# One PSUM bank of the attention stage handed from the score ring to the transposed-score ring

## The chip, the cores and the metric

The kernel runs on one core of one Trainium2 chip. The metric is the device time of one execution in microseconds (us); lower is better. The engines are TensorE (PE; PEld is its weight load), VectorE (DVE), ScalarE (ACT), GpSimd (POOL) and SyncE (SP), which issues the DMAs.

## What is computed

One pre-norm transformer block on x of shape (2, 1024, 512), fp32: attention with 16 heads of 32, rotary embedding and a causal mask, then a gated feed-forward with an inner width of 1408.

```python
def _L0_attn_ref(x, Wq, bq, Wk, bk, Wv, bv, Wo, bo):
    Q = proj(Wq, bq); K = proj(Wk, bk); V = proj(Wv, bv)
    Q = Q * cos + _rotate_half(Q) * sin
    K = K * cos + _rotate_half(K) * sin
    scores = jnp.einsum('bhqd,bhkd->bhqk', Q, K) / scale
    scores = jnp.where(causal, scores, jnp.float32(-jnp.inf))
    attn = jax.nn.softmax(scores, axis=-1)
    out = jnp.einsum('bhqk,bhkd->bhqd', attn, V)
    return out.transpose(0, 2, 1, 3).reshape(B, S, H) @ Wo.T + bo
...
x = x + _L0_attn_ref(_layernorm(x, axis=-1), ...)
x = x + _L0_ffn_ref(_layernorm(x, axis=-1), ...)
```

## The kernel before, in words

The program has three stages. Stage A (chunks of 512 tokens, four of them) normalises, transposes and projects to Q, K and V, rotates Q and K, and writes them to DRAM split into high and low parts. The attention stage goes over 32 heads (2 batches of 16). Stage C makes the output projection and the feed-forward.

In attention each head's scores are computed twice. First the plain scores, queries on partitions: `score_bank(u, i)` (L1034, matmul L1050) makes bank entry i of head u, and VectorE takes the row maximum out of it in `max_piece` (L769; L783 where the causal mask cuts it, L785 where not). A head has 12 entries: 0 to 4 are 512 columns wide, entry 5 (`M_ENTRY`) is no scores but the place of the transpose of the negated maxima (`transpose_max`, L1055), 6 to 8 are 384 wide, 9 and 10 are 256 wide and 11 holds two pieces of 256. `negate_max` (L789) turns the maxima of a head into 16 columns of `neg_max` in three small steps, placed behind entries 0, 1 and 2 of the next head; ScalarE copies the transposed maxima out (L663) and two DMAs put them beside the head's Q as extra contraction rows.

Second the transposed scores, keys on partitions, with the maximum already subtracted by those extra rows: `shifted_piece(t, i)` (L1116, matmul L1124) makes piece i of head t (12 pieces, 256 to 512 wide), and ScalarE takes the exponential out of it into `p32` (`exp_piece`, L645, activation L649). GpSimd clears the diagonal blocks (L529). `output_products` (L1127, matmul L1143) then multiplies p by V for a pair of heads; a pair's 24 matmuls stand in four groups of 8, 4, 6 and 6, called G0 to G3 here. In the profile each of them shows as two records, so G0 is "x16", G1 "x8", G2 and G3 "x12". ScalarE copies the accumulated outputs out of bank 7 (L656).

The order on TensorE is written out by hand in `b_step(t)` (L1148): for i from 0 to 11 it issues the score entry i of head t+2 (or the transpose of the maxima at i = 5), then the transposed piece i of head t, and after i = 3 and i = 9 a group of output products of the pair before. G0 and G1 stand in an even step t, G2 and G3 in an odd one. So between two groups TensorE issues either the entries 4 to 9 ("the middle stretch") or the entries 10 and 11 of one step and 0 to 3 of the next ("the long stretch"). In the first chunk of work, `early` (L1063, L804) puts the scores of heads 0 and 1 between the last products of stage A.

PSUM has eight banks of 512 fp32 columns. In attention the score entries go round `S_RING` banks from `S_BANK`, the transposed pieces round `ST_RING` banks from `ST_BANK`, and bank 7 holds the outputs. Each ring is guarded by a wait on TensorE ahead of the matmul, and whatever stands behind the waiting instruction waits too: entry i of the scores waits until VectorE is done with entry i - S_RING, piece i of the transposed scores until ScalarE is done with piece i - ST_RING:

```python
                elif i >= S_RING:
                    pe.wait_ge(s_max, NS * u + s_before(i - S_RING) + 1)
...
                if t > 0 or i >= ST_RING:
                    pe.wait_ge(exp_done, NPC * t + i - ST_RING + 1)
```

The transposed maxima lie in the score ring too (`M_BANK`); the entry that comes into that bank next, number 5 + S_RING, waits for ScalarE's copy of them (`max_T`, L1040). `transpose_max` waits for the entry that was in the bank ahead of it (L1058).

Of the kernel before, what the change touches and what calls it, by code (L numbers as in the profile page):

```python
# [109 lines left out]
def transformer_block(nc, x, wq, wk, wv, wo, bqk, bv, bo, ffn, gs, us, ds, cos, sin, shift_rows, out):  # L110
    ctx = ExitStack()
    with ctx:
# [99 lines left out]

        ps = ctx.enter_context(nc.psum_tensor("ps", [P, 8, 512], F32))
        T_BANK, MM_BANK, FLAG_BANK = 0, 4, 5
        S_BANK, ST_BANK, O_BANK = 0, 4, 7
        S_RING, ST_RING = 4, 3
        M_BANK = S_BANK + M_ENTRY % S_RING


# [1076 lines left out]
```

## Time and profile before

| what | value |
|---|---|
| median of 3 runs | 792.36 us (786.74 to 794.88) |
| the profiled execution, its own time | 785.66 us |
| its span, first to last instruction | 784.0 us |
| granted TensorE clock, mean over the span | 0.991 of full speed |
| PE busy | 740.0 us (94%) |
| PEld busy | 538.9 us (69%) |
| DVE busy | 436.1 us (56%) |
| ACT busy | 301.5 us (38%) |
| POOL busy | 243.2 us (31%) |

The span and the views of the trace belong to the profiled execution; 1.7 us of its time lie outside the span. Matmul records of the trace overlap, since each has a start, a streaming time and a drain; how fast TensorE goes is read from the distance between starts, not from the durations.

### The profile page before, as it was taken

How to read it: one execution, taken by the hardware profiler on the slowest of the kernel's cores; microseconds unless marked ns; L12 is line 12 of the kernel's file. 1: busy time of each engine (PE TensorE's matmuls, PEld its weight loads, DVE VectorE, ACT ScalarE, POOL GpSimd, SP SyncE). 2: the span in 40 equal slices, each digit the busy share in tenths (PEclk: the TensorE clock that was granted, in tenths of full speed). 3: DMA queues.
4: the chain of work that ended last, by engine and by line, in shares of the span. 5: the costliest groups of instructions: out<-in, count | busy, mean ns of one | idle time of the engine just before them, and what ended most of it. 6: DMA issues, size and time to landing. Idle time of an engine off the chain costs nothing.

```text
span 784.0 us, 10619 instructions
## 1 busy us (share of the span) xinstructions
PE 740.0 (94%) x3521; PEld 538.9 (69%) x3521; DVE 436.1 (56%) x1103; ACT 301.5 (38%) x637; POOL 243.2 (31%) x222
## 2 busy tenths in 40 slices
PE   3989899998999999999999998998999999999996
PEld 3768687876555555555555545887888888888885
DVE  6846575678777777777777733794114214214112
ACT  3231313137555555555555564222222223223221
POOL 0333333431113241414141415851123223123223
PEclk9999999999999999999999999999999999999998
DMA  8275479454557665757565545680001001001001
GB/s 275 85 265 215 162 246 309 187 196 138 153 161 185 160 179 154 188 157 190 154 186 152 139 124 165 228 348 2 0 1 54 1 0 54 0 0 54 1 0 56
DMA packets 52013, 104.37 MB, mean 133 GB/s; under 512 B 14821, under 2 KB 15333, under 8 KB 51445
## 3 DMA queue, kind: packets, MB, share of 16 engines
q1 hardware_dynamic: 51960, 103.72, 43.2%
q8 instruction: 27, 0.44, 0.2%
q14 instruction: 26, 0.20, 0.1%
HBM read 69.62 MB, written 38.21 MB: 138 GB/s over the span
## 4 chain that ended last, share of the span: by engine, by line
PE 79%; DVE 6%; issue 5%; ACT 4%; DMA 3%; SPq 1%; POOL 1%; ACTq 0%; DVEq 0%; POOLq 0%
PE ps L1026 32%; PE ps L1143 17%; PE ps L1219 10%; PE ps L1050 9%; PE ps L1124 9%; ACT p L649 1%; PE ps L1018 1%; DMA x_st<-in_x 1%; ACT o_raw L656 1%; DMA us_sb<-in_us 1%; DVE x L960 1%; ACT xT_hi L575 1%; DVE stats L969 1%; DVE oT_lo L933 1%; DVE xn L745 0%
## 5 line engine op out<-in xcount | busy, mean ns | idle before, releaser
L649 ACT ACTIVATE p<-ps 128x384 f32<-128x384 f32 (+3 forms) x384 | 162.2, 489 | 124.5 <-PE ps L1124 124.1
L783 DVE CUSTOM_DVE_ANT_0 masked<-ps,mask_qk 128x512 bf16<-128x512 f32 (+1 forms) x240 | 115.4, 503 | 74.8 <-PE ps L1050 72.2
L1124 PE MATMUL ps<-q_st,k_st 99*128 99x384 f32 (+2 forms) x384 | 135.6, 371 | 6.7 <-ACT p L649 6.6
L1143 PE MATMUL ps<-p,v_slot 128*64 128x512 f32 (+3 forms) x768 | 137.5, 493 | 2.2 <-ACT o_raw L656 2.1
L1050 PE MATMUL ps<-k_st,q_st 96*128 96x512 f32 (+2 forms) x384 | 131.3, 363 | 1.1 <-DVE row_max L783 0.9
L985 DVE SCALAR_TENSOR_TENSOR hid<-ps,us_sb,silu 128x512 f32<-128x512 f32 x44 | 33.0, 750 | 169.0 <-PE ps L1026 166.5
L560 POOL TENSOR_TENSOR hid_lo<-hid,hid_hi 128x512 fp32r<-128x512 f32 x44 | 56.8, 1290 | 175.2 <-ACT hid_hi L720 175.2
L529 POOL TENSOR_SCALAR_AFFINE_SELECT p<-p 128x512 f32<-128x512 f32 x64 | 40.5, 635 | 208.7 <-ACT p L649 208.5
L1143 PEld LDWEIGHTS ps<-p,v_slot 128*64 128x64 f32 x768 | 52.6, 136 | 74.6 <-issue 61.8
L1050 PEld LDWEIGHTS ps<-k_st,q_st 96*128 96x128 f32 x384 | 72.9, 191 | 30.3 <-issue 21.6
L1124 PEld LDWEIGHTS ps<-q_st,k_st 99*128 99x128 f32 x384 | 72.9, 191 | 26.3 <-ACT p L649 15.9
L785 DVE TENSOR_REDUCE row_max<-ps 128x1 f32<-128x512 f32 (+1 forms) x128 | 83.1, 651 | 0.1
L1026 PE MATMUL ps<-xT_hi,wg_sb 128*128 128x512 f32 x176 | 68.6, 390 | 2.9 <-DVE x L960 2.9
L1219 PE MATMUL ps<-wd_sb,hid_hi 128*128 128x512 f32 x176 | 69.1, 393 | 0.0
L1219 PE MATMUL ps<-wd_sb,hid_lo 128*128 128x512 f32 x176 | 68.5, 389 | 0.0
L1026 PE MATMUL ps<-xT_lo,wg_sb 128*128 128x512 f32 x176 | 68.5, 389 | 0.0
L1026 PE MATMUL ps<-xT_lo,wu_sb 128*128 128x512 f32 x176 | 68.5, 389 | 0.0
L1026 PE MATMUL ps<-xT_hi,wu_sb 128*128 128x512 f32 x176 | 68.5, 389 | 0.0
L717 ACT ACTIVATE silu<-ps,gs_sb 128x512 f32<-128x512 f32 x44 | 30.4, 690 | 88.6 <-PE ps L1026 88.6
L499 POOL TENSOR_TENSOR rot<-ecos,osin 128x512 f32<-128x512 f32 x16 | 28.0, 1747 | 109.4 <-DVE ocos L840 109.4
L720 ACT CAST hid_hi<-hid 128x512 fp32r<-128x512 f32 x44 | 27.4, 623 | 83.1 <-DVE hid L985 83.1
L606 ACT CAST st_hi<-rot 128x1024 fp32r<-128x1024 f32 x16 | 17.0, 1060 | 88.8 <-POOL rot L500 77.5
(94 smaller groups left out, 1063.8 us busy)
## 6 DMA issues: line engine op xcount, KB each, us to landing
qk_scratch<-st_hi SPq DMA_DIRECT2D x32, 512.0 KB, 3.8
q_st<-qk_scratch SPq DMA_DIRECT2D x32, 384.0 KB, 4.1
k_st<-qk_scratch SPq DMA_DIRECT2D x32, 384.0 KB, 5.5
flag_st<-in_ffn SPq DMA_DIRECT2D x32, 264.0 KB, 2.8
ffn_copy<-in_ffn SPq DMA_DIRECT2D x32, 264.0 KB, 3.4
qk_scratch<-st_lo SPq DMA_DIRECT2D x16, 512.0 KB, 4.1
o_T<-o_raw SPq DMA_DIRECT2D x32, 128.0 KB, 4.0
rec_l<-rec_rows SPq DMA_DIRECT2D x32, 128.0 KB, 3.3
```

The source lines that it names most:

```text
L529: pool.affine_select(out=diagonals, in_=diagonals, compare_op=ALU.is_ge, fill=0.0, base=0, pattern=[[0, KT // 2], [1, P]], channel_multipl ...
L560: pool.tensor_tensor(hid_lo[:, i % 3, :], hid[:, i % 2, :], hid_hi[:, i % 3, :].bitcast(F32), ALU.subtract).then_inc(hid_lo_done, 1)
L649: act.activation(p32[:, at:at + q0 + w - keep], ps[:, ST_BANK + i % ST_RING, keep - q0:w], ACT.Exp, scale=SCALE).then_inc(exp_done, 1)
L717: act.activation(silu[:, i % 2, :], ps[:, T_BANK + 2 * (i % 2), :], ACT.Silu, scale=gs_sb[:, i:i + 1]).then_inc(silu_ready, 1)
L783: ins = dve.tensor_tensor_reduce((masked_a if u < 2 else masked)[:, s_before(i) % 2, col:col + kept], scores, mask_qk[:, 512 - kept:512], ...
L785: ins = dve.tensor_reduce(dst, scores, AX_X, ALU.max)
L985: dve.scalar_tensor_tensor(out=hid[:, i % 2, :], in0=ps[:, T_BANK + 2 * (i % 2) + 1, :], scalar=us_sb[:, i:i + 1], in1=silu[:, i % 2, :], ...
L1026: ins = pe.matmul(dst, w, m, start=(k == 0), stop=(k == len(terms) - 1))
L1050: ins = pe.matmul(ps[:, S_BANK + i % S_RING, col:col + w], q_st[0:K_DOT, slot, qt * P:(qt + 1) * P], k_st[0:K_DOT, slot, k0:k0 + w], start ...
L1124: pe.matmul(ps[:, ST_BANK + i % ST_RING, 0:w], k_st[0:K_ALL, slot, kt * P:(kt + 1) * P], q_st[0:K_ALL, slot, q0:q0 + w], start=True, stop= ...
L1143: ins = pe.matmul(ps[VW * a:VW * (a + 1), O_BANK, q0 - 512 * half:512], v_slot[:, slot, kt, :], p32[:, at:at + n], start=(kt == 0), stop=( ...
L1219: ins = pe.matmul(ps[:, MM_BANK + j, :], t(h[:, i % 3, tile]), t(wd_sb[:, i, :]), start=(i == 0 and k == 0), stop=(i == IT - 1 and k == 1))
```

## The change

The score ring gets banks 0 to 2 instead of 0 to 3, and the ring of the transposed scores banks 3 to 6 instead of 4 to 6. Everything else follows by the formulas: an entry of the scores waits for the entry three places before it, not four, a transposed piece for the exponential four places before it, not three, the transposed maxima move from bank 1 to bank 2, and the entry that waits for their copy is 8, not 9. The order of instructions on every engine is the same.

```diff
         T_BANK, MM_BANK, FLAG_BANK = 0, 4, 5
-        S_BANK, ST_BANK, O_BANK = 0, 4, 7
-        S_RING, ST_RING = 4, 3
+        S_BANK, ST_BANK, O_BANK = 0, 3, 7
+        S_RING, ST_RING = 3, 4
         M_BANK = S_BANK + M_ENTRY % S_RING
```

## Rows read from the trace of the kernel before

**Rows 1.** Busy time and granted clock by stretch of time: one at half clock, the steady part.

```profile
core 0: us, PE busy (x) PEld busy (x) DVE busy (x) ACT busy (x) POOL busy (x), PEclk, DMA share, GB/s
...
186.00:189.00 3.00, 3.00 (x10) 2.45 (x9) 2.72 (x13) 1.92 (x4) 1.61 (x3) 0.51 0.81 214
...
228.00:456.00 228.00, 223.43 (x1171) 133.03 (x1171) 164.57 (x581) 131.60 (x335) 68.83 (x83) 1.00 0.64 166
```

**Rows 2.** Who waited for whom, 174 to 478 us: total, times, longest.

```profile
PEld ps L1124 <- ACT p L649: 15.9, 38, 0.8
...
PE ps L1050 <- DVE row_max L783: 0.6, 1, 0.6
```

**Rows 3.** TensorE's timeline (start us, us), even step's middle stretch, from entry 4.

```profile
268.39 0.50 PE L1050 MATMUL ps<-k_st,q_st 96*128 96x512 f32 x1
...
269.48 0.34 PE L1050 MATMUL ps<-k_st,q_st 96*128 96x384 f32 x1
...
269.92 0.33 PE L1050 MATMUL ps<-k_st,q_st 96*128 96x384 f32 x1
270.63 0.39 PE L1124 MATMUL ps<-q_st,k_st 99*128 99x256 f32 x1 [0.38 <-ACT p L649]
...
270.97 0.28 PE L1124 MATMUL ps<-q_st,k_st 99*128 99x256 f32 x1
271.19 1.94 PE L1143 MATMUL ps<-p,v_slot 128*64 128x512 f32 x8
```

**Rows 4.** Timeline of VectorE, the same stretch: entry 4.

```profile
269.03 0.69 DVE L783 CUSTOM_DVE_ANT_0 masked<-ps,mask_qk 128x512 bf16<-128x512 f32 x1 [0.86 <-PE ps L1050]
269.65 0.08 DVE L783 DVE_READ_ACCUMULATOR2_ANT row_max<- 128x1 f32 x1
```

**Rows 5.** Timeline of ScalarE, the same stretch: exponential 4, an output copy, exponentials 5 to 9.

```profile
269.10 0.49 ACT L649 ACTIVATE p<-ps 128x384 f32<-128x384 f32 x1 [1.78 <-PE ps L1124]
...
269.63 0.57 ACT L656 COPY o_raw<-ps 128x512 f32<-128x512 f32 x1
270.11 1.61 ACT L649 ACTIVATE p<-ps 128x384 f32<-128x384 f32 x5
```

**Rows 6.** Timeline of TensorE, middle stretch of an odd step: entries 4, 7, G3.

```profile
277.92 0.50 PE L1050 MATMUL ps<-k_st,q_st 96*128 96x512 f32 x1
...
279.02 0.34 PE L1050 MATMUL ps<-k_st,q_st 96*128 96x384 f32 x1
...
280.25 2.15 PE L1143 MATMUL ps<-p,v_slot 128*64 128x512 f32 x12
```

**Rows 7.** Timelines of TensorE, its weight load and VectorE, end of a long stretch.

```profile
284.55 0.40 PE L1050 MATMUL ps<-k_st,q_st 96*128 96x512 f32 x1
284.78 0.40 PE L1124 MATMUL ps<-q_st,k_st 99*128 99x512 f32 x1
285.15 0.65 PE L1143 MATMUL ps<-p,v_slot 128*64 128x512 f32 x2
...
284.37 0.19 PEld L1050 LDWEIGHTS ps<-k_st,q_st 96*128 96x128 f32 x1
...
283.90 0.69 DVE L785 TENSOR_REDUCE row_max<-ps 128x1 f32<-128x512 f32 x1
```

**Rows 8.** Timelines at the start of attention: TensorE and VectorE, and a wait.

```profile
163.53 0.88 PE L1050 MATMUL ps<-k_st,q_st 96*128 96x256 f32 x5
...
164.31 0.08 DVE L783 DVE_READ_ACCUMULATOR2_ANT row_max<- 128x1 f32 x1
...
184.81 0.08 DVE L783 DVE_READ_ACCUMULATOR2_ANT row_max<- 128x1 f32 x1
...
184.94 0.19 PEld L1050 LDWEIGHTS ps<-k_st,q_st 96*128 96x128 f32 x1 [0.93 <-DVE row_max L783]
```

**Rows 9.** Timeline of TensorE's weight load, steps 30 and 31.

```profile
461.29 0.34 PEld L1124 LDWEIGHTS ps<-q_st,k_st 99*128 99x128 f32 x2 [0.81 <-ACT p L649]
...
465.69 0.19 PEld L1124 LDWEIGHTS ps<-q_st,k_st 99*128 99x128 f32 x1 [0.30 <-ACT p L649]
```

## The prediction

> **What bounds the kernel now.** I read the windows by stage first. From 228 to 456 us, the steady part of attention, TensorE is busy 223.43 of 228 us at full clock, VectorE 164.57 (72%), ScalarE 131.60 (58%) [rows 1]. So the instruction stream of TensorE sets the time, and the two engines that empty the rings have slack on average. What is left to ask is where TensorE stands still, since nothing on it shortens: the edit removes and adds no instruction. The sums of waits name both rings: transposed pieces waited for ScalarE 15.9 us at the weight load, in 38 places, scores for VectorE hardly at all [rows 2]. By that list alone the change moves a bank from the ring that never waits to the one that does. But a sum of waits shows only what is late with four score banks. Whether three are enough must be read from the timelines, by putting the third predecessor's end beside each entry's start. I did that for one pair of heads, two steps; a step takes 277.92 - 268.39 = 9.53 us from entry 4 to entry 4 [rows 3, 6], and the pattern repeats.
>
> **The constants of the walk.** (a) A wait that ends shows in the weight load: VectorE's piece ended at 184.81 + 0.08 = 184.89, the weight load behind it began at 184.94, so 0.05 us from end to release [rows 8]. (b) A matmul whose weight load came late takes 0.11 us longer: the same 256-wide form has 0.39 after a wait and 0.28 without [rows 3]. Otherwise the load starts 0.18 us or so ahead of its matmul (284.37 for 284.55 [rows 7]). (c) Starts without a stall lie 0.23 us apart behind a 512-wide piece (284.55 to 284.78 [rows 7]). By the same full-clock rate I take 0.18 behind a 384-wide and 0.12 behind a 256-wide one. The last piece ahead of a group of output products has 0.22 (270.97 to 271.19 [rows 3]) or 0.37 (284.78 to 285.15 [rows 7]).
>
> **Long stretch, entries 10, 11, 0 to 3, in which TensorE starts an entry every 0.4 to 0.47 us.** VectorE needs 0.69 for a 512-wide one [rows 7]. Entry 3 now waits for entry 0, not for entry 11. VectorE ended entry 0 at 283.90 + 0.69 = 284.59 [rows 7]. The weight load can start at 284.64, and the matmul streams from 284.75 where it started at 284.55: +0.20 us for TensorE, and the transposed piece and the output group queued behind it move along. Entries 0, 1 and 2 wait for 9, 10 and 11, which end in time or within some hundredths. There are two such stretches in a pair: +0.40. Bounds: 0 if the load of the next weights hides it, 0.30 each where VectorE has the reciprocals of a group ahead.
>
> **Middle stretch, entries 4 to 9.** Entry 7 now waits for entry 4, and only four entries are left between two groups. Entry 4 starts at 268.39 [rows 3], VectorE takes it up at 269.03 and is done at 269.65 + 0.08 = 269.73 [rows 4]. Entry 7 started at 269.48; now its weight load starts at 269.78 and it streams from 269.89, 0.41 late.
> In the even step there was a wait that this one replaces. Piece 8 of the transposed scores stood until 270.63 [rows 3] because exponential 5 comes behind the output copy at 269.63 and starts only at 270.11 [rows 5]. With four banks piece 8 waits for exponential 4, over by 269.59. From 269.89 the walk is: piece 7 at 270.07, entry 8 at 270.25, piece 8 at 270.43, entry 9 at 270.55, piece 9 at 270.67. But piece 9 now is the one that waits for exponential 5: weight load at 270.63, streaming from 270.74, G1 at 270.74 + 0.22 = 270.96 instead of 271.19. So the removed wait comes back one piece later and only 0.23 us are won (bounds: none won; 0.43 if entry 7 did not wait at all, and then the wait of piece 9 still stands, so 0.23 again).
> In the odd step ScalarE makes no output copy there and there is little to win. Entry 4 starts at 277.92, 1.39 later the weight load of entry 7 is free (279.31, for 269.78 - 268.39 = 1.39), it streams from 279.42 instead of 279.02 [rows 6]; piece 7 at 279.60, entry 8 at 279.78, piece 8 at 279.96, entry 9 at 280.08, piece 9 at 280.20, G3 at 280.42 instead of 280.25: +0.17. The small ScalarE waits of this stretch (part of the 15.9 [rows 2]) are in that difference. Bounds: -0.2 if VectorE were no obstacle, +0.41 if nothing is given back.
> The moved bank of the maxima costs nothing: entry 8 waits for their copy, which stands on ScalarE between exponential 4 and the output copy, so is over before 269.63 + the release, ahead of 270.25. The transpose itself waits for entry 2 instead of 1, which VectorE ends well before the group of output products is through.
>
> **Per pair:** 0.40 + 0.17 - 0.23 = +0.34 us. Steps 2 to 29 have both scores and output products, 14 pairs: **+4.8 us.**
>
> **Start of attention.** (1) Between stage A's last products five matmuls of scores (entries 9, 10, 11, and 0 of the next head) go out at once from 163.53, 0.12 apart [rows 8]. The last would now wait for entry 9, which VectorE ends at 164.31 + 0.08 [rows 8]: streaming from 164.55 where it was 163.53 + 4 x 0.12 = 164.01, +0.54, and VectorE waits for the next scores after it, so nothing absorbs it. (2) In step 1, which has no output products, VectorE is the bound and entry 8 waited for entry 4 until 184.94 [rows 8]. Now entry 7 stands there, with piece 7 and entry 8 behind it, 0.28 + 0.18 - 0.11 = +0.35. Together **+0.9** (0 to 2).
> **End of attention.** Steps 30 and 31 have no scores, only the fourth transposed bank counts. The waits for an exponential (the first and second of them in [rows 9], a third in step 31) fall on the piece after: about 0.1 before G1 of step 30 (the piece behind is the last), 0.5 (one exponential, 0.49 [rows 5]) before G2, 0.2 before G3: **-0.8** (-1.5 to 0). What follows, output copy and DMAs, hangs on G3 and moves with it. Stage C has no ring of this kind.
>
> **Sum:** 4.8 + 0.9 - 0.8 = +4.9 us. Against the profiled execution 785.66 + 4.9 = 790.6; that execution is 6.7 us under the median of the three runs, and I put the same difference on the median: 792.36 + 4.9 = **797.3 us**, 0.6% slower. A measurement of this kernel can tell about 1% from no change, so the likeliest verdict is no difference.
>
> **Rivals.**
> A. *The score waits are hidden and only ScalarE's go.* For it: VectorE is idle 28% of the steady part and scores never waited [rows 1, 2]. Then a pair wins 0.23 + 0.20, 14 pairs 6.0, the end 0.8: -6.8 us, 785.6. Against it: the load of entry 7 cannot start before VectorE's end at 269.73, and that end follows entry 4's own start by a fixed 1.34 us [rows 3, 4], however idle VectorE is. Chance 0.14.
> B. *Every score wait adds in full, nothing is given back.* Place: the four stretches of a pair; price 2 x 0.30 + 2 x 0.41 = 1.42, x 14 = 20 us, +0.9: 813. It decides where the piece behind a late entry waits for ScalarE anyway, i.e. if exponentials slide along with TensorE. For it: exponentials 5 to 9 are close behind one another, 1.61 us for five [rows 5]. Against it: the ScalarE wait of 270.63 is set by the output copy, which starts by G0's end, not by entry 7. In weaker form (half of it, +10) it lies in the range. Chance 0.16.
> C. *TensorE's clock falls.* After TensorE stood still in steps 0 and 1, the granted clock was 0.51 of full speed from 186 to 189 us [rows 1], that is 1.2 GHz. In these 3 us about half the work got done, 1.5 us lost. If the added stops brought such a stretch in each pair: 14 x 1.5 = 21 us on top, 818. Against it: the new stops are 0.2 to 0.4 us, like the one at 270.63 behind which the clock stayed at 1.00. Chance 0.06.
> The Trainium skill (TensorE: Matmul & The Clock Gate, "A second HAM failure mode: psum-queue depth-cycling") says that a kernel which cycles through PSUM banks can idle TensorE in small bits often enough for the clock to swing. By that rule this change, with more small stops, would be case C; the steady part with its 15.9 us of small waits at clock 1.00 [rows 1, 2] speaks against it.
> D. *The change does nothing*, because gain and loss cancel stretch by stretch: within 1.5 us of 792.4. It needs the long stretch to hide its 0.2; it is part of the forecast's own range.
>
> **How the numbers follow.** Forecast with D 0.64 (from -1 to +9 us), A 0.14, B 0.16, C 0.06. Faster by over 1% (under 784.4) only in the far part of A and by the spread of the runs: 0.07. Slower by over 1% (over 800.3): C, most of B and the edge of the forecast, 0.24. Within 1%: 0.69. The runs before spread over 8 us by themselves. Range: from A's 786 to half of B, 792.4 + 13 = 806, with C and full B left out.
>
> **What would show it.** In a steady pair: a wait of entry 7 for VectorE (masked piece, L783) of about 0.4 us at the weight load in both middle stretches, one of entry 3 for the unmasked maximum (L785) of 0.2 to 0.3 in both long ones, in sum 15 to 20 us of new waits at L1050; ScalarE's waits at L1124 down from 15.9 to a few us, the rest on piece 9 of even steps; the pair longer by 0.34 us, VectorE's and ScalarE's busy times and the clock unchanged. Wrong would be: no waits at L1050 in the middle stretches (A), the wait of piece 8 still there in even steps (B), half-clock stretches between 208 and 456 us (C).

## The result and the profile after

The changed kernel takes 793.90 us (median of 17 runs, 789.03 to 800.96), the kernel before 788.15 us in the same comparison (17 runs, 783.90 to 794.88): ratio 1.0069, 95% interval 1.0046 to 1.0091. The ratio leaves out the one run of 800.96 us, which is over 1.5% above the fastest of its kernel. So it is 0.7% slower, within the 1% forecast as no difference; the text put it at 0.6%. The profiled execution took 793.90 us with a span of 792.2 us, 8.2 us more than the profiled one of before.

The page of the changed kernel has VectorE, ScalarE and GpSimd within 5 us of before, PE 11.8 us higher:

```profile
PE 751.8 (95%) x3521; PEld 537.3 (68%) x3521; DVE 440.9 (56%) x1103; ACT 303.1 (38%) x637; POOL 243.5 (31%) x222
```

The windows of the changed kernel (columns as in [rows 1]), the start of attention first, then the steady part:

```profile
186.00:189.00 3.00, 2.85 (x12) 2.63 (x13) 2.52 (x12) 1.64 (x4) 0.64 (x1) 0.73 0.56 172
190.00:192.00 2.00, 2.00 (x6) 1.32 (x5) 1.84 (x7) 1.59 (x3) 0.60 (x2) 0.50 0.84 262
192.00:194.00 2.00, 2.00 (x5) 0.53 (x6) 1.31 (x3) 0.60 (x2) 0.00 (x0) 0.50 0.40 133
228.00:456.00 228.00, 224.03 (x1148) 126.61 (x1144) 162.29 (x567) 130.64 (x328) 69.24 (x83) 1.00 0.63 167
```

In the last row TensorE seems busier than before (224.03 against 223.43), and yet it starts 1148 matmuls in that time instead of 1171: a matmul whose weights come late has a longer record, so busy time hides the small stops. The count tells better: 2.0% fewer, of which a part can be records missing from the trace. The clock stays at 1.00 there. From 188 to 194 us it is 0.50, that is 1.2 GHz; before, the stretch at this level was shorter and over by 190 us.

The sums of waits, 174 to 478 us, of the changed kernel:

```profile
PEld ps L1050 <- DVE row_max L783: 19.1, 61, 0.9
...
PEld ps L1050 <- DVE row_max L785: 9.7, 32, 0.4
...
PEld ps L1124 <- ACT p L649: 2.8, 8, 0.8
...
PEld ps L1124 <- DMA q_st<-neg_max_T: 1.3, 2, 1.0
```

The last row is TensorE waiting for the DMAs that carry the maxima. The 15.9 us at the transposed pieces [rows 2] are down to 2.8, and 28.8 us at the scores, where before there was next to nothing, stand in their place. As in the forecast, these sums don't subtract to the change in time: most of a wait is taken back by the next one that falls away.

Where a wait costs, only the distances between groups of output products tell. This table is read from TensorE's timeline, distances between the starts of the groups of one pair of heads in steady state (the pair from G0 at 266.08 us before, at 270.66 after), in us:

| stretch | before | after | difference | forecast |
|---|---|---|---|---|
| G0 to G1 (even middle) | 5.11 | 4.88 | -0.23 | -0.23 |
| G1 to G2 (long) | 4.64 | 4.92 | +0.28 | +0.20 |
| G2 to G3 (odd middle) | 4.42 | 4.57 | +0.15 | +0.17 |
| G3 to G0 (long) | 4.90 | 5.05 | +0.15 | +0.20 |
| sum | 19.07 | 19.42 | +0.35 | +0.34 |

The steady pairs of the changed kernel take 19.42 and 19.35 us in turn; they differ in G1 to G2, 4.92 in one and 4.84 in the next. Where it is 4.92, VectorE has the reciprocals of a group of heads ahead of the maxima, and entry 2 of the scores waits 0.25 us where it otherwise waits 0.17:

```profile
278.29 0.35 DVE L904 RECIPROCAL l_cols<-l_cols 128x32 f32<-128x32 f32 x1
...
279.18 0.19 PEld L1050 LDWEIGHTS ps<-k_st,q_st 96*128 96x128 f32 x1 [0.25 <-DVE row_max L783]
```

TensorE's timeline of the changed kernel in that pair: the even middle stretch from entry 4 to G1, the odd one from entry 4 to G3, entry 3 at the end of the next long one. It answers to [rows 3, 6, 7].

```profile
272.96 0.50 PE L1050 MATMUL ps<-k_st,q_st 96*128 96x512 f32 x1
...
274.37 0.44 PE L1050 MATMUL ps<-k_st,q_st 96*128 96x384 f32 x1
...
275.24 0.37 PE L1124 MATMUL ps<-q_st,k_st 99*128 99x256 f32 x1
275.54 1.94 PE L1143 MATMUL ps<-p,v_slot 128*64 128x512 f32 x8
...
282.54 0.50 PE L1050 MATMUL ps<-k_st,q_st 96*128 96x512 f32 x1
...
283.95 0.44 PE L1050 MATMUL ps<-k_st,q_st 96*128 96x384 f32 x1
...
285.03 2.15 PE L1143 MATMUL ps<-p,v_slot 128*64 128x512 f32 x12
...
289.42 0.50 PE L1050 MATMUL ps<-k_st,q_st 96*128 96x512 f32 x1
289.75 0.40 PE L1124 MATMUL ps<-q_st,k_st 99*128 99x512 f32 x1
```

The weight loads of the same instructions, with the wait in brackets (idle time, and who ended it):

```profile
274.36 0.19 PEld L1050 LDWEIGHTS ps<-k_st,q_st 96*128 96x128 f32 x1 [0.40 <-DVE row_max L783]
...
283.95 0.19 PEld L1050 LDWEIGHTS ps<-k_st,q_st 96*128 96x128 f32 x1 [0.40 <-DVE row_max L783]
...
288.81 0.19 PEld L1050 LDWEIGHTS ps<-k_st,q_st 96*128 96x128 f32 x1 [0.17 <-DVE row_max L783]
289.42 0.19 PEld L1050 LDWEIGHTS ps<-k_st,q_st 96*128 96x128 f32 x1 [0.30 <-DVE row_max L785]
```

And VectorE's timeline beside them: entry 4 of the even step, and entry 0 (unmasked) ahead of the last wait.

```profile
273.61 0.69 DVE L783 CUSTOM_DVE_ANT_0 masked<-ps,mask_qk 128x512 bf16<-128x512 f32 x1 [1.03 <-PE ps L1050]
274.23 0.08 DVE L783 DVE_READ_ACCUMULATOR2_ANT row_max<- 128x1 f32 x1
...
288.68 0.69 DVE L785 TENSOR_REDUCE row_max<-ps 128x1 f32<-128x512 f32 x1
```

Entry 4 starts at 272.96, its maximum ends at 274.23 + 0.08 = 274.31, and the weight load of entry 7 begins at 274.36: 0.05 us later, 1.40 us after entry 4's start (the forecast had 1.39). The odd step repeats it: 282.54 to 283.95 is 1.41. In the long stretch entry 0's maximum ends at 288.68 + 0.69 = 289.37 and entry 3's load begins at 289.42. From entry 4 to G1 it takes 2.58 us instead of 2.80 [rows 3], from entry 4 to G3 2.49 instead of 2.33 [rows 6].

**Where the 8.2 us of the profiled execution are.** Worked out from starts on TensorE (before, after): stage A reached the first score at 139.93 and 138.22 us (-1.7, which no edit explains); first score to first transposed piece 34.41 and 37.24 (+2.8); from there to the first G0 15.48 and 16.80 (+1.3); from it to the next G0 19.07 and 20.28 (+1.2); then 12 pairs 229.05 and 233.89 (+4.8); then to the first group of output products behind step 31, 36.37 and 35.65 (-0.7); after it +0.5. The sum is 8.2. The start of attention is the part that the forecast did not see: 2.83 + 1.32 + 1.21 = 5.4 us, where 0.9 was written. Putting TensorE's starts of the two kernels beside each other splits it: 2.8 are there at the first transposed piece, 3.3 at the end of step 1, of which about 0.35 is step 1's own, as forecast; 0.3 is that of one regular pair; the other 1.8 come in while the clock is at 1.2 GHz, which lasts longer after the change.

The changed kernel's timelines in stage A's last chunk, where scores stand one by one between groups of twelve products. TensorE:

```profile
154.83 0.44 PE L1050 MATMUL ps<-k_st,q_st 96*128 96x384 f32 x1 [1.58 <-DVE row_max L785]
...
164.69 0.47 PE L1050 MATMUL ps<-k_st,q_st 96*128 96x512 f32 x1 [0.37 <-DVE row_max L783]
```

VectorE:

```profile
152.96 1.22 DVE L849 TENSOR_TENSOR st_lo<-rot,st_hi 128x1024 fp32r<-128x1024 f32 x1
154.09 0.69 DVE L785 TENSOR_REDUCE row_max<-ps 128x1 f32<-128x512 f32 x1
```

The second TensorE row is the wait in the burst [rows 8], foreseen. The first was not. Entry 6 of head 0 now waits for entry 3, and since entry 5 is no scores, only entry 4 goes out between them. Entry 3 started at 147.14; VectorE takes its maximum only behind the four products of the rotation and the low parts (L849), and is done at 154.09 + 0.69 = 154.78. Entry 6 would be due two places of 2.97 us after entry 3, at 153.08, and starts at 154.83, 1.75 late. In the kernel before it waited for entry 2, taken ahead of the rotation:

```profile
151.82 0.40 PE L1050 MATMUL ps<-k_st,q_st 96*128 96x512 f32 x1
...
154.79 0.34 PE L1050 MATMUL ps<-k_st,q_st 96*128 96x384 f32 x1
```

It comes out 2.97 us behind entry 4, with no wait.

### The profile page after: what moved, and what is told of

It is laid out like the page before. It is cut to its first block, busy times and chain, and to the rows that moved or that the text cites. A ratio compares the mean times of both kernels' runs of the same rounds, so it can differ in the third digit from the quotient of the medians.

```text
span 792.2 us, 10619 instructions
## 1 busy us (share of the span) xinstructions
PE 751.8 (95%) x3521; PEld 537.3 (68%) x3521; DVE 440.9 (56%) x1103; ACT 303.1 (38%) x637; POOL 243.5 (31%) x222
## 4 chain that ended last, share of the span: by engine, by line
PE 80%; DVE 7%; issue 5%; DMA 2%; ACT 2%; SPq 1%; POOL 1%; DVEq 0%; POOLq 0%; ACTq 0%
PE ps L1026 34%; PE ps L1143 16%; PE ps L1050 11%; PE ps L1219 10%; PE ps L1124 7%; DVE masked L783 2%; PE ps L1018 1%; DVE x L960 1%; DMA us_sb<-in_us 1%; ACT xT_hi L575 1%; DMA q_st<-neg_max_T 1%; DVE stats L969 1%; DVE oT_lo L933 1%; DVE row_max L783 0%; POOL o_T L520 0%
## 5 line engine op out<-in xcount | busy, mean ns | idle before, releaser
L783 DVE CUSTOM_DVE_ANT_0 masked<-ps,mask_qk 128x512 bf16<-128x512 f32 (+1 forms) x240 | 114.7, 503 | 77.7 <-PE ps L1050 76.3
L1050 PE MATMUL ps<-k_st,q_st 96*128 96x512 f32 (+2 forms) x384 | 139.5, 383 | 8.0 <-DVE row_max L783 1.9
L1124 PE MATMUL ps<-q_st,k_st 99*128 99x384 f32 (+2 forms) x384 | 131.0, 360 | 1.4 <-DMA q_st<-neg_max_T 0.7
L1050 PEld LDWEIGHTS ps<-k_st,q_st 96*128 96x128 f32 x384 | 73.0, 191 | 58.2 <-issue 22.1
L529 POOL TENSOR_SCALAR_AFFINE_SELECT p<-p 128x512 f32<-128x512 f32 x64 | 40.8, 639 | 217.1 <-ACT p L649 217.1
L1143 PEld LDWEIGHTS ps<-p,v_slot 128*64 128x64 f32 x768 | 50.2, 137 | 78.7 <-issue 67.4
```

Source lines behind the costliest of these rows:

```text
L529: pool.affine_select(out=diagonals, in_=diagonals, compare_op=ALU.is_ge, fill=0.0, base=0, pattern=[[0, KT // 2], [1, P]], channel_multipl ...
L783: ins = dve.tensor_tensor_reduce((masked_a if u < 2 else masked)[:, s_before(i) % 2, col:col + kept], scores, mask_qk[:, 512 - kept:512], ...
L1050: ins = pe.matmul(ps[:, S_BANK + i % S_RING, col:col + w], q_st[0:K_DOT, slot, qt * P:(qt + 1) * P], k_st[0:K_DOT, slot, k0:k0 + w], start ...
L1124: pe.matmul(ps[:, ST_BANK + i % ST_RING, 0:w], k_st[0:K_ALL, slot, kt * P:(kt + 1) * P], q_st[0:K_ALL, slot, q0:q0 + w], start=True, stop= ...
L1143: ins = pe.matmul(ps[VW * a:VW * (a + 1), O_BANK, q0 - 512 * half:512], v_slot[:, slot, kt, :], p32[:, at:at + n], start=(kt == 0), stop=( ...
```

## The experiments

The theory going in: the loss is the waits of entries 7 and 3 (and what the start adds), the gain is the even middle stretch and the end, and both are read as in the forecast. The rivals: the scores' waits cost nothing and something else made it slower; or the change moved the clock. "Pair" below is G0 to G0 in steady state.

**1. Only take the bank away from the scores** (kernel before, ring of three, bank 3 unused).

```diff
-        S_RING, ST_RING = 4, 3
+        S_RING, ST_RING = 3, 3
```

> Both rings three banks deep, the transposed scores in banks 4 to 6 as before, bank 3 unused: the loss of the change without its gain. Theory (VectorE's waits cost, ScalarE's fourth bank gives back 0.23 us in even steps only): per pair +0.40 in the two long stretches, +0.17 in the odd middle stretch and 0 in the even one, where the late entry 7 hides behind the ScalarE wait of piece 8, which still ends at the same place; 14 pairs +8.0, start of attention as in the changed kernel (+1 to +3.7), no gain at the end: +9 to +12 us, ratio 1.012 to 1.015. Rival (the fourth bank of the transposed scores gives nothing, the loss is all in the score ring): as the changed kernel, 1.007.

Measured: 798.99 us (6 runs) against 787.88, ratio 1.0140 (1.0116 to 1.0164). A pair takes 19.59 to 19.67, +0.55 on 19.07. In the even middle stretch both waits are there, the one for VectorE and then the old one for ScalarE:

```profile
276.52 0.19 PEld L1050 LDWEIGHTS ps<-k_st,q_st 96*128 96x128 f32 x1 [0.40 <-DVE row_max L783]
277.37 0.19 PEld L1124 LDWEIGHTS ps<-q_st,k_st 99*128 99x128 f32 x1 [0.38 <-ACT p L649]
```

So the fourth score bank is worth 0.55 a pair, and the fourth transposed bank gives 0.55 - 0.32 = 0.23 of it back: the two halves of the forecast, each by itself. Entry 6 in stage A stands 1.58 us here too, and first score to first transposed piece is 37.21 (142.13 to 179.34), so the score ring alone makes that loss. The clock, however, stood at 1.00 from 180 to 204 us: the half-clock stretch did not come with the ring of three alone.

**2. Take away the wait that the transposed bank was to cure, in the kernel before.** ScalarE copies the outputs one place earlier, ahead of exponential 4 instead of behind it, so that exponential 5 is not late.

```diff
-                    if t % 2 == 0 and t >= 2 and i == PV_AFTER[0][0] + 1:
+                    if t % 2 == 0 and t >= 2 and i == PV_AFTER[0][0]:
```

> Kernel before, but ScalarE takes the output copy (L656, half 0) ahead of exponential 4 instead of behind it; it waits for G0, and ScalarE stood idle there for 1.78 us. Theory (the 0.48 us of this copy between exponentials 4 and 5 is what the fourth bank buys off in even steps): the wait of piece 8 goes, G1 at 270.78 instead of 271.19, 0.41 in each of 15 even steps: -6 us, ratio 0.992. Rival (the copy only moves the wait to exponential 4, since G0's last product drains late): ratio 1.000.

Measured: 782.47 us (10 runs) against 787.88, ratio 0.9938 (0.9916 to 0.9959). It beats both kernels. Its ScalarE in an even step:

```profile
265.90 0.59 ACT L656 COPY o_raw<-ps 128x512 f32<-128x512 f32 x1 [1.18 <-PE ps L1143]
266.52 0.49 ACT L649 ACTIVATE p<-ps 128x384 f32<-128x384 f32 x1
266.90 0.24 ACT L663 COPY neg_max_T<-ps 16x128 f32<-16x128 f32 x1
267.05 1.33 ACT L649 ACTIVATE p<-ps 128x384 f32<-128x384 f32 x4
```

The copy now fills idle time (1.18 us ahead of it), and nothing stands between exponentials 4 and 5 but the short copy of the maxima. G0 to G1 takes 4.64 us instead of 5.11, a pair 18.60 instead of 19.07. Of these 0.47 a pair, 14 x 0.47 = 6.6 us, 5.4 arrive in the median; a likely place for the rest is a row of this kernel's waits, 228 to 456 us, that the forecast had no word on:

```profile
PEld ps L1124 <- DMA q_st<-neg_max_T: 4.3, 6, 1.4
```

TensorE gets to the transposed piece before the DMAs that carry the transposed maxima to Q's extra rows have landed. Every second pair takes 18.85 to 19.80 for that.

**3. The same edit in the changed kernel.**

> The same edit in the changed kernel. Theory: its even middle stretch is set by entry 7 waiting for VectorE, and the copy holds up only piece 9 by 0.07 to 0.1 us: -1 to -1.5 us against the changed kernel, ratio to before 1.005 to 1.006. Rival (ScalarE's order is worth the same with any rings): -6 us there too, ratio to before 0.999.

Measured: 795.41 us (9 runs) against 787.88, ratio 1.0078 (1.0051 to 1.0104). The pair is 19.25 to 19.33, 0.10 less than after, which the median does not show. In the changed kernel the copy's place is worth 0.1 a pair, in the kernel before 0.47. The score ring differs too, so the difference is not the transposed bank's alone: entry 7's wait for VectorE stands in the same stretch. But bank and order both act on the wait of piece 8 behind the output copy, and only the order costs no score bank.

**4 to 6. Shorten what the score entries wait for.** VectorE takes the maximum over the first 256 columns only, for entries 0 and 4 in the kernel before (4), for entry 4 alone in the changed one (5), for entry 0 alone in the changed one (6). These three leave out half of the columns of those entries' maxima.

```diff
                         kept = min(w, P * (qt + 1) - k0)
+                        kept = min(kept, 256) if i in (0, 4) else kept
```

> Kernel before, with the row maximum of entries 0 and 4 of each head taken over 256 of their 512 columns (the other half is left out of the maximum). Control for the two cuts in the changed kernel. Theory: with four score banks no score waits for VectorE outside steps 0 and 1, so 0.54 us less VectorE work per head gives nothing in the steady part and at most 1 to 2 us at the start: ratio 0.998 to 1.000. Rival (VectorE's work itself sets the pace): -7 us or more, 0.991.

> Changed kernel, row maximum of entry 4 over 256 of its 512 columns (the other half left out). Theory: entry 7's wait in the middle stretch falls from 0.40 to about 0.13 us; in odd steps G3 comes 0.27 earlier, in even steps nothing is won because piece 9 then still waits for exponential 5 behind the output copy: 14 x 0.27 = -3.8 us against the changed kernel, ratio to before about 1.002. Rival (entry 7's wait costs in both steps): -7.5 us, 0.997.

> Changed kernel, row maximum of entry 0 over 256 of its 512 columns (the other half left out). Theory: entry 3's wait for entry 0 (0.30 us at the weight load) goes in both long stretches of a pair, entry 2's small wait for entry 11 stays: -0.2 to -0.3 each, 28 of them, -6 to -8 us against the changed kernel, ratio to before 0.997 to 0.999. Rival (the long stretches are bound by the sum of VectorE's work ahead of entry 11, or by the first weight load of the output products): -2 us or less, 1.005.

Measured, with the ratio to the kernel before: (4) 786.63 us, 0.9988 (0.9964 to 1.0012), undisturbed pair 19.07 as ever: with four score banks nobody waits for these maxima in the steady part. (5) 791.75 us, 1.0029 (1.0005 to 1.0053), pair 19.20 to 19.27, 0.15 less than after, nearly all of it between G2 and G3 (4.44 for 4.57, where before has 4.42), half of the 0.27 expected. (6) 789.80 us, 1.0017 (0.9995 to 1.0039), pair 19.00 to 19.07, 0.36 less than after, where 0.4 to 0.6 was expected. In (6) both long stretches are back at 4.64 to 4.72 and 4.90 us, the middle ones stay at 4.87 and 4.57. So the long stretches carry the whole loss of a pair, and the middle ones together are a small gain (-0.23 + 0.15), as the table above has it. In (6) entry 3's wait is gone and entry 2's is left (the added line of the edit makes L1050 L1051 here, and L783 L784):

```profile
294.71 0.19 PEld L1051 LDWEIGHTS ps<-k_st,q_st 96*128 96x128 f32 x1 [0.17 <-DVE row_max L784]
```

That 0.17 at entry 2 costs nothing, since this stretch is 4.65 as before; in the pairs with 4.72 the wait is 0.25, so about 0.07 of it is paid. In (5) the wait of entry 7 is gone, but piece 9 still comes behind exponential 5:

```profile
274.08 0.19 PEld L1125 LDWEIGHTS ps<-q_st,k_st 99*128 99x128 f32 x1 [0.15 <-ACT p L649]
```

This is the floor of the forecast's even middle stretch ("0.23 again" if entry 7 did not wait), and why the edit gave back less than the two waits of 0.40.

The profiled execution of (4) had five longer pairs, 19.59 to 22.23 us. The longest holds a wait for the landing of the maxima and behind it a stretch in which the clock fell (0.50 from 256 to 258 us), so that twelve records of output products took 3.85 us for some 2.2:

```profile
252.90 0.50 PE L1125 MATMUL ps<-q_st,k_st 99*128 99x512 f32 x1 [1.21 <-DMA q_st<-neg_max_T]
...
254.68 3.85 PE L1144 MATMUL ps<-p,v_slot 128*64 128x512 f32 x12
```

**7. One bank fewer still** (changed kernel, ring of two, one execution).

```diff
-        S_RING, ST_RING = 3, 4
+        S_RING, ST_RING = 2, 4
```

> Score ring two banks deep, ring of the transposed scores four. The dose one step further, and a test whether many small stops bring TensorE's clock down. An entry waits for the second before it, whose maximum ends 1.34 us after its start, so 512-wide entries come 0.7 to 0.8 us apart instead of 0.47: about +1.3 to +1.8 us in a long stretch and +0.7 to +1.2 in a middle one, +4 to +6 us per pair, 840 to 875 us. Clock: by my theory still 1.00 in the steady part; by the rival (small stops let it fall) stretches at half clock between 228 and 456 us, and a time above 880.

Measured: 864.18 us, of one execution. Its windows, the start, then a steady stretch, then one of the 18 us pieces with a lower clock:

```profile
182.00:206.00 24.00, 23.33 (x62) 14.78 (x63) 17.26 (x56) 14.13 (x30) 3.23 (x6) 0.50 0.37 112
228.00:318.00 90.00, 83.24 (x387) 41.14 (x387) 56.74 (x189) 47.18 (x109) 17.47 (x24) 1.00 0.50 137
...
318.00:336.00 18.00, 16.33 (x63) 7.14 (x65) 13.52 (x37) 9.33 (x21) 7.79 (x7) 0.91 0.56 150
```

A pair takes 23.0 us, +3.9, at clock 1.00 through 90 us in which TensorE stood 6.8 us in small stops. With two banks there are twelve waits for a maximum in a pair, 0.17 to 0.74 us each (42.0 us at L1050 for L783 from 228 to 456). Going from four to three costs 0.55 a pair, from three to two 3.6. The clock of the steady part fell here three times, each time near a single stop of TensorE of 1.0 to 1.3 us (matmuls at 325.26, 373.49 and 422.25). That is not peculiar to the short ring: with four score banks it fell once in the profiled execution of (4), once in (8) and twice in (10), each time beside a single stop of 1.2 to 3.1 us. Stops of 1.2 to 1.4 us in (5) and (9) left it at 1.00, so the length of a stop alone does not decide it.

**8 to 12. Follow the new limit of experiment 2.** All on the kernel before with its edit. (8) ScalarE's copy of the transposed maxima also goes one place later, behind exponential 5. (9) Not that, but the DMA of the reciprocals (`load_rec`) is issued one step later, out of the way of the maxima's DMAs. (10) Both. (11) As (9), and GpSimd scales the outputs in step t % 4 = 1 behind its masks. (12) As (11) with (8)'s edit.

```diff
-M_AFTER = 4
+M_AFTER = 5
...
-                if t % 4 == 3 and t >= 7:
-                    load_rec((t - 7) // 4)
+                if t % 4 == 0 and t >= 8 or t == HEADS - 1:
+                    load_rec((t - 7) // 4 if t == HEADS - 1 else (t - 8) // 4)
...
-                if t % 4 == 0 and t >= 8:
-                    scale_group((t - 8) // 4)
                 mask_p(t)
+                if t % 4 == 1 and t >= 9:
+                    scale_group((t - 9) // 4)
```

> Kernel before with the output copy (L656, half 0) ahead of exponential 4 and the copy of the transposed maxima (L663) behind exponential 5 instead of 4. Theory: exponential 5 comes 0.15 us earlier, so piece 8's remaining wait of 0.1 to 0.2 us goes in both kinds of step: a further -1 to -3 us beyond the moved output copy alone, ratio to before 0.988 to 0.992. Rival (nothing waits there any more, or entry 9 now waits for the copy of the maxima): as the moved output copy alone or up to 0.5% slower than it.

> Kernel before with the output copy ahead of exponential 4, and the loads of the reciprocals (L419, 4 x 128 KB, once in four heads) issued one step later, behind that step's load of the maxima. With the output copy moved alone, steady pairs took 18.60 us instead of 19.07, but every second pair lost 0.2 to 1.2 us more, waiting at piece 0 of the transposed scores for the landing of the maxima (q_st<-neg_max_T). Theory (those DMAs queue behind the reciprocals' loads and the head loads issued just ahead of them): the extra waits go, all pairs at 18.60, 3 to 4 us less than with the copy alone, ratio to before 0.988 to 0.991. Rival (the waits come from the head loads and the output moves alone, or move to GpSimd's masks, which now stand behind a later scaling): no gain or a loss, 0.994 or more.

> The same with the copy of the transposed maxima (L663) behind exponential 5. Without the later reciprocals this had steady pairs of 18.43 us, 0.17 less than the output copy alone, and lost it all to later landings of the maxima. Theory (the landing is what limits both): a gain of up to 14 x 0.17 = 2.4 us over the kernel with the copy of the maxima behind exponential 4 only if the landing waits are gone there; since this edit sends the maxima 0.4 us later, I expect between -2 and +2 us against that kernel, ratio to before 0.986 to 0.993.

> Kernel before with the output copy ahead of exponential 4, the reciprocals' loads one step later, and GpSimd's scaling of a group (L518, L520, 5.2 us) behind the masks of the step after instead of ahead of the masks of its own step. With the later loads alone the landing waits of the maxima were gone (0.4 us left of 4.3), but the scaling came 8 us later and pushed the masks behind it, and G0 waited about 1 us for them in every second pair. Theory: with the scaling behind the masks nothing of this is left and all steady pairs take 18.60 us: 14 x 0.47 = 6.6 us less than before, ratio 0.989 to 0.993, and below the output copy alone (0.994). Rival (another landing or the masks still come late): some pairs above 19, 0.995 or more.

> The same with the copy of the transposed maxima behind exponential 5. Its undisturbed pair is 18.43 us. Theory: if the landings stay in time, 14 x 0.64 = 9 us less than before, 0.987 to 0.990; since the maxima leave 0.4 us later I give even odds that head loads and maxima land late in some pairs and it ends where the kernel without this edit does or above, 0.990 to 0.996.

The medians of before beside them are 788.45 us (8), 787.68 (9, 10) and 787.84 (11, 12).

| run | median us (runs) | ratio to before, interval | undisturbed pair | what disturbs the others |
|---|---|---|---|---|
| 2 | 782.47 (10) | 0.9938, 0.9916 to 0.9959 | 18.60 | landing of the maxima, 4.3 us |
| 8 | 784.38 (12) | 0.9953, 0.9920 to 0.9987 | 18.43 | landing of the maxima, 7.0 us; the clock falls once |
| 9 | 785.55 (12) | 0.9976, 0.9953 to 1.0000 | 18.60 | G0 waits for p, 8.3 us |
| 10 | 790.88 (12) | 1.0014, 0.9989 to 1.0040 | 18.44 | G0 waits up to 3.1 us for the masks, and the clock falls twice; pairs of 19.8 to 21.6 |
| 11 | 783.69 (8) | 0.9953, 0.9926 to 0.9981 | 18.60 | VectorE held up by GpSimd |
| 12 | 781.79 (8) | 0.9927, 0.9883 to 0.9970 | 18.43 | the same, and one landing wait |

The expectations of 8 to 11 were missed, those of 8, 9 and 11 on the side of their rivals and that of 10 beyond its range: the undisturbed pairs came out as expected, and what disturbs the others was larger. In 12 the worse of its two branches came. The later copy of the maxima shortens the undisturbed pair by 0.17, and in (8) more is lost than that at the DMAs that start later by it, in the one execution profiled. In (9) the waits for the maxima's landing are nearly gone (0.4 us), so the reciprocals' DMA was in their way, but GpSimd, which scales the outputs with those reciprocals, now begins with a wait and blocks its own masks:

```profile
255.33 2.38 POOL L518 TENSOR_TENSOR o_T<-o_T,rec_l 128x1024 f32<-128x1024 f32 x1 [12.30 <-DMA rec_l<-rec_rows]
257.81 2.85 POOL L520 TENSOR_SCALAR o_T<-o_T,bv_sb 128x1024 f32<-128x1024 f32 x1
```

and TensorE waits for the masked p at G0:

```profile
262.99 0.23 PEld L1143 LDWEIGHTS ps<-p,v_slot 128*64 128x64 f32 x4 [1.60 <-ACT p L649]
```

The row names ScalarE; by the order on GpSimd it is rather the masks (L529), which start only at 260.61, behind the scaling. In (10) the scaling starts still later and the same wait reaches 3.1 us. In (11), where the scaling stands behind the masks, this wait is gone. Experiment 12 has the lowest ratio, but its interval overlaps that of 2, so which of the two is faster is open. Experiment 2 is one line and beats both kernels.

## Why the prediction was right

**The constants held.** Release 0.05 us behind the maximum's end, matmul 0.10 us longer after a late load, where 0.11 was taken (0.50 in place of the 0.40 of entry 3 [rows 7], 0.44 in place of 0.34 for a 384-wide entry [rows 3]), 1.40 us from an entry's start to the load that waits for it. The pair was forecast at +0.34; the mean of ten regular pairs after is 19.39, +0.32.

**Long stretch, +0.20 each.** Measured +0.28 and +0.15, together 0.43 for 0.40. Experiment 6 pins it on entry 0's maximum. In every second pair the first is +0.20, as written; the +0.28 stands where VectorE has the reciprocals ahead, which the forecast had as its bound of 0.30.

**Even middle stretch, -0.23, odd +0.17.** Measured -0.23 and +0.15. Experiment 1 shows the wait for ScalarE still there with three transposed banks, experiment 5 shows the rest of it at piece 9, both as the forecast's walk has them.

**Start of attention, +0.9: the term that was mis-sized.** First score to first transposed piece is +2.8 us, and it is so in each profiled kernel with three score banks (37.2 in experiments 1, 3, 5, 6) against 34.4 in each with four (2, 4, 8 to 12). The forecast gave 0.54 for this stretch, for the burst at 163.53 [rows 8], and the burst did cost 0.53. The entries that go out one by one ahead of it, some 2.9 us apart, have no term in it and no reason why not; they cost 1.85, and two waits behind the burst make up the rest. Between entries 3 and 6 there are only two places, 5.9 us, and VectorE does not serve the scores at once: the rotation is ahead of them in its queue, and entry 3's maximum ended 7.6 us after its start. The same wait of 1.58 us stands at entry 6 in the changed kernel and in experiments 1, 3, 5 and 6. The rule (put the third predecessor's end beside each start) was right, and was applied at one place too few. With 2.8 in place of 0.54 the sum is 4.8 + 2.8 + 0.35 - 0.8 = 7.2 us for a difference of medians of 5.75. So it is partly luck that 4.9 came so near 5.75: the missing 2.3 us at the start were offset by something that no run isolates. The time itself, 797.3, is 3.4 us above the 793.90 measured, because the 792.36 it starts from was the median of three runs, and that of 17 is 788.15. The bound of 2 for this term was too low as well.

**End, -0.8.** From the G0 of step 30 (before at 456.97, after at 465.55) the four stretches to the next groups took 4.79, 4.36, 3.97 and 4.22 us before and 4.64, 3.87, 3.81 and 4.21 after: -0.15, -0.49, -0.16 and -0.01, for the forecast's 0.1, 0.5, 0.2. The waits for an exponential that are left at the weight loads (they answer to [rows 9]):

```profile
469.87 0.19 PEld L1124 LDWEIGHTS ps<-q_st,k_st 99*128 99x128 f32 x1 [0.81 <-ACT p L649]
...
473.63 0.19 PEld L1124 LDWEIGHTS ps<-q_st,k_st 99*128 99x128 f32 x1 [0.20 <-ACT p L649]
...
477.55 0.19 PEld L1124 LDWEIGHTS ps<-q_st,k_st 99*128 99x128 f32 x1 [0.19 <-ACT p L649]
```

**What the forecast had no term for.** In the profiled execution two of the 12 steady pairs were longer than the rest (20.31 and 19.70), together 1.2 us, the first for the landing of the maxima, the second for VectorE, whose maxima came 0.26 us later behind the reciprocals than in the other pairs; before, one was (19.31, landing). Taken as regular, 13 x 0.32 = 4.2, with 2.8 + 0.35 at the start and -0.7 from the last pair on is 6.6 us. The interval of the ratio is 3.6 to 7.2 us, so it holds this and the 5.75 between the medians. That the rest of the profiled 8.2 us (half-clock stretch, longer pairs, stage A's -1.7) is scatter of single executions is argued, not shown.

**The rivals.** A (scores' waits hidden) fell with 28.8 us of waits at L1050 and with experiments 1 and 6. B (every wait adds in full) fell with -0.23 in the even middle stretch. C: the steady part kept its clock in the profiled execution of the changed kernel, at 1.00 through 228 us with small stops of 0.2 to 0.4 us and one of 0.67 (ahead of 298.99). What the Trainium skill's passage on depth-cycling (TensorE: Matmul & The Clock Gate, "A second HAM failure mode: psum-queue depth-cycling") tells of one kernel, a clock that swings with small stops, this trace does not show at this size of stops. Experiment 7, with more and longer ones, held 1.00 for 90 us and then showed windows of 0.91. There, as in 4, 8 and 10, a single stop of a microsecond or more stands beside each fall; what sets it off is open. At the start, behind the idle steps 0 and 1, the stretch at 1.2 GHz was longer in the changed kernel and made its first G0 take 3.32 us for 2.38:

```profile
192.26 3.32 PE L1143 MATMUL ps<-p,v_slot 128*64 128x512 f32 x16
```

Experiment 1, with the same score ring, has no such stretch. But each of the four profiled kernels with rings of 3 and 4 (after, 3, 5, 6) has a mean granted clock of 0.86 from 174 to 198 us, where the kernel before, 2 and 11 have 0.93 and 1, 4, 8, 9, 10 and 12 have 1.00 (7, with a ring of two, 0.64). With one execution each this points to the change and doesn't show it; how the rings would do it is open. It can't be much in the medians: the mean granted clock is 0.988 over the 17 runs of after and 0.989 over the 24 of before beside experiment 1. D (nothing) is excluded by the interval, though the measured ratio is small.

**Left open.** Whether stage A's loss could be had back by taking entry 3's maximum ahead of the rotation was not tried; nor a ring of three with entry 0's maximum split in two.

## What to carry to other kernels

A ring's depth is tested entry by entry: set the end of the consumer's work on entry i - depth beside the start of entry i, in every phase in which the ring runs, also where the consumer has another job in its queue (here the rotation in stage A: 1.85 us of the 2.8 at the start, a third of the whole difference). A sum of waits does not name the bank to move: the ring that never waited lost 0.55 us a pair when it lost its fourth bank, and the one that waited 15.9 us gave back 0.23. Ask first what makes the wait late: one side job of the consumer moved by one place won 0.6%, where a bank for the same wait lost 0.7%.

## What the runs showed of the hardware

**GpSimd locked VectorE out of a small operation.** In experiment 11 VectorE's subtraction on 128 x 8 elements, 0.17 us elsewhere (0.17 in the changed kernel at 289.96), stood beside GpSimd's scaling. VectorE:

```profile
262.23 1.85 DVE L798 TENSOR_SCALAR neg_max<-max 128x8 fp32r<-128x8 f32 x1
264.00 0.68 DVE L785 TENSOR_REDUCE row_max<-ps 128x1 f32<-128x512 f32 x1
```

GpSimd:

```profile
261.69 2.37 POOL L518 TENSOR_TENSOR o_T<-o_T,rec_l 128x1024 f32<-128x1024 f32 x1
```

It ends at 264.08, with GpSimd's at 264.06, so it was held until the other was through. The same subtraction took 1.85 us at five places some 38 us apart; the maxima out of PSUM, beside GpSimd's next instruction, kept their 0.68. TensorE then waits 0.93 us for a later maximum (weight load at 267.17), and every second pair, from the fifth on, is 19.7 us. The Trainium skill (SBUF — State Buffer, "Who interferes with whom") tells of an exclusive lock on a port pair that the two engines share, taken for a whole instruction by whoever issues first; this trace agrees.

**A DMA of a few KB became the limit.** In experiment 2 the two small DMAs of the maxima, 16 x 128 elements together, landed too late in 6 places, for up to 1.4 us. Issuing the reciprocals' DMA one step later nearly took these waits away: 0 to 0.9 us from 228 to 456 us in experiments 9 to 12, against 4.3 in 2 and 7.0 in 8. A shorter pair is not needed for them: (4), with pairs of 19.07, had 5.3 us, the kernel before 0.3 and after 1.3. So they differ from execution to execution, and how much of them the medians carry is not shown.
